# A four-block Mamba, sign and expert kernel: normalised outputs joined to the residual in one VectorE operation, their means carried to the end

## The reference

```python
x = x + _layernorm(_L0_attn_ref(_layernorm(x), ...))   # selective scan, 16 states
x = x + _layernorm(_L0_ffn_ref(_layernorm(x), ...))    # sign(x) @ sign(w).T, bias, alpha
x = x + _layernorm(_L1_attn_ref(_layernorm(x), ...))   # selective scan again
x = x + _layernorm(_L1_ffn_ref(_layernorm(x), ...))    # 16 experts, top 2, and 2 shared
```

## Time and profile before

| | us |
|---|---|
| median of 3 runs (791.62 to 793.70) | 792.56 |
| the profiled execution | 792.4 |
| its span | 790.5 |
| VectorE busy | 574.4 |
| TensorE busy (matmul) | 653.1 |

### The profile page before, as it was taken

The page is one execution under the profiler, slowest core; times in us unless marked ns, Lnnn a source line. Parts: engine busy times, 40 slices in busy tenths (PEclk is TensorE's granted clock), DMA queues, the critical chain, the costliest instruction groups (busy, mean ns, idle before and its releaser), DMA issues.

```text
span 790.5 us, 10083 instructions
## 1 busy us (share of the span) xinstructions
PE 653.1 (83%) x2907; PEld 417.3 (53%) x2909; DVE 574.4 (73%) x1137; ACT 542.5 (69%) x1213; POOL 453.2 (57%) x396
## 2 busy tenths in 40 slices
PE   3936999999994438648999999984989999999960
PEld 2325555555552324234555555543867777777640
DVE  6365999999997585649999999979583134444358
ACT  2769999999986775959999999956323322222225
POOL 0034999999994131048999999955047423333400
PEclk9956999999997577968999999995599999999986
DMA  6031444444430000012535444417012323333163
GB/s 165 6 67 36 133 140 133 140 133 142 131 115 1 0 1 3 18 58 94 149 118 160 134 134 149 131 46 231 1 54 94 105 96 107 106 105 103 64 219 107
DMA packets 57567, 77.65 MB, mean 98 GB/s; under 512 B 8113, under 2 KB 38481, under 8 KB 57521
## 3 DMA queue, kind: packets, MB, share of 16 engines
q1 hardware_dynamic: 53728, 66.75, 28.0%
q0 software_dynamic: 3792, 10.36, 3.7%
HBM read 58.21 MB, written 18.87 MB: 98 GB/s over the span
## 4 chain that ended last, share of the span: by engine, by line
PE 74%; DVE 13%; ACT 7%; POOL 3%; DMA 2%; issue 1%; SPq 0%; ACTq 0%; POOLq 0%; DVEq 0%
PE bank L1060 28%; PE bank L1050 14%; PE bank L1097 11%; DVE st L342 4%; PE bank L1105 3%; PE bank L1106 3%; PE bank L948 2%; PE bank L951 2%; POOL arena L896 2%; PE bank L961 2%; PE bank L934 2%; PE bank L970 2%; DVE tok_a L381 1%; ACT rings L793 1%; PE bank L1167 1%; DVE rings L686 1%
## 5 line engine op out<-in xcount | busy, mean ns | idle before, releaser
L881 POOL TENSOR_TENSOR arena<-arena,rings 128x512 f32<-128x512 f32 x256 | 321.6, 1283 | 31.3 <-DVE arena L510 26.9
L510 DVE TENSOR_TENSOR_SCAN arena<-rings,bank 128x512 f32<-128x512 f32 x256 | 296.2, 1200 | 15.9 <-PE bank L1050 7.1
L1060 PE MATMUL bank<-arena,ident 128*128 128x512 f32 x512 | 263.7, 601 | 0.0
L1050 PEld LDWEIGHTS bank<-ident,rings 128*128 128x128 f32 x1024 | 131.3, 145 | 143.8 <-issue 124.6
L793 ACT ACTIVATE rings<-tok_a,b_tok 128x256 f32<-128x256 f32 x448 | 191.0, 495 | 0.4 <-ACT tok_a L753 0.4
L803 ACT ACTIVATE rings<-arena,a_sb 128x512 f32<-128x512 f32 x256 | 169.1, 709 | 0.0
L1050 PE MATMUL bank<-ident,rings 128*128 128x128 f32 x1024 | 158.4, 280 | 11.3 <-ACT rings L793 10.9
L918 POOL DMA_INDIRECT y_tok<-rings,dest x47 | 44.9, 955 | 82.9 <-DVE rings L659 82.6
L1060 PEld LDWEIGHTS bank<-arena,ident 128*128 128x128 f32 x512 | 79.3, 193 | 5.7 <-issue 4.8
L857 ACT ACTIVATE silu<-bank 128x176 f32<-128x176 f32 x47 | 14.9, 317 | 85.5 <-PE bank L1097 85.5
L896 POOL TENSOR_TENSOR arena<-arena,feat_a 128x512 f32<-128x512 f32 x8 | 18.7, 2357 | 90.1 <-DVE arena L402 90.1
(11 more groups left out here) (160 smaller groups left out, 852.8 us busy)
## 6 DMA issues: line engine op xcount, KB each, us to landing
rings<-c_rows SPq DMA_DIRECT2D x128, 256.0 KB, 3.3
w_sb<-w SPq DMA_DIRECT2D x18, 352.0 KB, 4.1
x_sorted<-zeros SPq DMA_DIRECT2D x47, 128.0 KB, 3.2
rings<-x_sorted SPq DMA_DIRECT2D x47, 128.0 KB, 2.0
arena<-w SPq DMA_DIRECT2D x2, 2048.0 KB, 12.3
residual<-x SPq DMA_DIRECT2D x4, 512.0 KB, 6.1
tok_a<-y_tok SPq DMA_DIRECT2D x4, 512.0 KB, 7.3
w_sb<-y_tok SPq DMA_DIRECT2D x4, 512.0 KB, 8.1
```

The costliest lines, as they stand in the source:

```text
L510: dve.tensor_tensor_scan(state[:, u % STATE_RING, :], abar[:, u % ABAR_RING, :], bank[u % B_RING][:, :], 0.0, ALU.mult, ALU.add).then_inc( ...
L881: pool.tensor_tensor(s, s, crep[:, k % CREP_RING, :], ALU.mult).then_inc(hc_ready, 1)
L1050: ins = pe.transpose(bank[u % B_RING][:, j * P:(j + 1) * P], v_ring[:, s % V_RING, j, h * P:(h + 1) * P], ident[:, :])
L1060: pe.matmul(ysum_of[b % 2][h][:, :], ident[:, :], state[:, u % STATE_RING, :], start=n == 0, stop=n == N - 1).then_inc(state_free, 1)
```

## The change

In `y_add` and `r_add` VectorE adds `f * rstd` to X in one scalar_tensor_tensor per chunk; ScalarE's normalise and GpSimd's add go, and the term `-mean * rstd` is not added to X. The moments and reciprocals of these three norms are kept in buffers of their own. Since `mean * rstd` is one number for a token, the norms that read X are not changed by it; the sum of the three is formed once, in `carry`, ahead of the expert loops, and joined to the shift of the last norm (`m_norm`), which has one operation more. `x_norm` leaves only the reciprocal on VectorE, and GpSimd does the four tensor_scalar of a quarter. `f_mm` moves from VectorE to ScalarE, as an activation with scale alpha and bias `bias * alpha`, a product formed once after the first scan.

```diff
+            def add_scale(name, q, l):
+
+                g = slice(q * CQ, (q + 1) * CQ)
+                dve.wait_ge(std_ready, stat_of[q])
+                f, x_added = (f_tok[l - 1], y_added) if name == "y_add" else (f_tok[0], r_added)
+                rstd = moments(name, l)[1]
+                done(dve.reciprocal(rstd[:, g], std[:, g]))
+                settle()
+                for c in range(q * CQ, (q + 1) * CQ):
+                    dve.scalar_tensor_tensor(X[:, c, :], f[:, c, :], rstd[:, c:c + 1], X[:, c, :], ALU.mult, ALU.add)\
+                       .then_inc(x_added, 1)
...
-                if name != "x_norm":
+                if name == "f_norm":
                     dve.scalar_tensor_tensor(shift[:, g], mom[:, g, 0], -1.0, rstd[:, g], ALU.mult, ALU.mult)\
+                       .then_inc(scale_ready, 1)
+                elif name == "m_norm":
+                    done(dve.tensor_tensor(shift[:, g], mom[:, g, 0], rstd[:, g], ALU.mult))
+                    settle()
+                    dve.scalar_tensor_tensor(shift[:, g], shift[:, g], -1.0, carry[:, g], ALU.mult, ALU.subtract)\
                        .then_inc(scale_ready, 1)
...
                 elif name == "x_norm":
-                    scale(name, q)
-                    for c in range(q * CQ, (q + 1) * CQ):
-                        dve.tensor_scalar(tok_a[:, c, :], X[:, c, :], mom[:, c, 0:1], rstd[:, c:c + 1], ALU.subtract,
-                                          ALU.mult).then_inc(norm_ready, 1)
+                    dve.wait_ge(std_ready, stat_of[q])
+                    dve.reciprocal(rstd[:, g], std[:, g]).then_inc(x_scale_ready, 1)
...
-                elif name == "f_mm":
-                    for h in range(H):
-                        dve.wait_ge(ffn_ready, q * H + h + 1)
-                        dve.tensor_scalar(feat_a[:, h, t], bank[4 + h][:, :], bias_sb[:, h:h + 1], alpha_sb[:, h:h + 1],
-                                          ALU.add, ALU.mult).then_inc(scaled, 1)
...
+            done(dve.tensor_tensor(bias_sb[:, :], bias_sb[:, :], alpha_sb[:, :], ALU.mult))
...
+            done(dve.tensor_tensor(carry[:, :], kept_mom[0][:, :, 0], kept_rstd[0][:, :], ALU.mult))
+            for i in (1, 2):
+                settle()
+                done(dve.tensor_tensor(carry_part[:, :], kept_mom[i][:, :, 0], kept_rstd[i][:, :], ALU.mult))
+                settle()
+                done(dve.tensor_tensor(carry[:, :], carry[:, :], carry_part[:, :], ALU.add))
...
-                elif name in ("y_add", "f_norm", "r_add", "m_norm"):
+                elif name in ("f_norm", "m_norm"):
                     normalise(name, q, l)
...
+                elif name == "f_mm":
+                    for h in range(H):
+                        act.wait_ge(ffn_ready, q * H + h + 1)
+                        act.activation(feat_a[:, h, t], bank[4 + h][:, :], ACT.Identity, scale=alpha_sb[:, h:h + 1],
+                                       bias=bias_sb[:, h:h + 1]).then_inc(scaled, 1)
...
-                if name in ("y_add", "r_add"):
-                    f, f_normed, x_added = (f_tok[l - 1], y_normed, y_added) if name == "y_add" else (f_tok[0], r_normed, r_added)
+                if name == "x_norm":
+                    pool.wait_ge(x_scale_ready, l * Q + q + 1)
                     for c in range(q * CQ, (q + 1) * CQ):
-                        n = ((l - 1) * C if name == "y_add" else 0) + c + 1
-                        pool.wait_ge(f_normed, n)
-                        pool.tensor_tensor(X[:, c, :], X[:, c, :], f[:, c, :], ALU.add).then_inc(x_added, 1)
+                        pool.tensor_scalar(tok_a[:, c, :], X[:, c, :], mom[:, c, 0:1], rstd[:, c:c + 1], ALU.subtract,
+                                           ALU.mult).then_inc(norm_ready, 1)
```

More of the change, by code:

```diff
@@ L143, in sandwich_kernel @@
         rstd, shift = sb("rstd", [P, C]), sb("shift", [P, C])
+        kept_mom = [sb(f"kept_mom{i}", [P, C, 2]) for i in range(3)]
+        kept_rstd = [sb(f"kept_rstd{i}", [P, C]) for i in range(3)]
+        carry, carry_part = sb("carry", [P, C]), sb("carry_part", [P, C])
         eps_sb = sb("eps_sb", [P, 1])
@@ L179, in sandwich_kernel @@
         ftr_ready, ftr_copied = sem("ftr_ready"), sem("ftr_copied")
-        y_normed, r_normed, m_normed, y_added, r_added = (
-            sem(n) for n in ("y_normed", "r_normed", "m_normed", "y_added", "r_added"))
+        m_normed, y_added, r_added = (
+            sem(n) for n in ("m_normed", "y_added", "r_added"))
         g_normed = sem("g_normed")
@@ L233, in norm_of, with moments @@
         def norm_of(name, l):
-            return {"y_add": (f_tok[l - 1], f_tok[l - 1], y_normed), "f_norm": (tok_a, X, g_normed),
-                    "r_add": (f_tok[0], f_tok[0], r_normed), "m_norm": (f_moe, f_moe, m_normed)}[name]
+            return {"f_norm": (tok_a, X, g_normed), "m_norm": (f_moe, f_moe, m_normed)}[name]
+        def moments(name, l):
+            i = {"y_": 2 * (l - 1), "r_": 1}.get(name[:2])
+            return (mom, rstd) if i is None else (kept_mom[i], kept_rstd[i])
         block = ctx.enter_context(nc.Block())
@@ L333, in settle, with stat @@
                 dve.wait_ge(dve_done, steps[0])
-            def stat(src, q, ready=None, count=0, each=1):
+            def stat(src, q, ready=None, count=0, each=1, mom=mom):
                 for c in range(q * CQ, (q + 1) * CQ):
@@ L406, in stage @@
                 elif name == "y_stat":
-                    stat(f_tok[l - 1], q, ytr_copied, ((l - 1) * Q + q) * 2, 2)
-                elif name == "y_add":
-                    scale(name, q)
+                    stat(f_tok[l - 1], q, ytr_copied, ((l - 1) * Q + q) * 2, 2, moments(name, l)[0])
+                elif name in ("y_add", "r_add"):
+                    add_scale(name, q, l)
                 elif name == "f_stat":
@@ L423, in stage @@
                     scale(name, q)
-                elif name == "f_mm":
-                    for h in range(H):
-                        dve.wait_ge(ffn_ready, q * H + h + 1)
-                        dve.tensor_scalar(feat_a[:, h, t], bank[4 + h][:, :], bias_sb[:, h:h + 1], alpha_sb[:, h:h + 1],
-                                          ALU.add, ALU.mult).then_inc(scaled, 1)
                 elif name == "r_stat":
-                    stat(f_tok[0], q, ftok_copied, q * 2, 2)
-                elif name == "r_add":
-                    scale(name, q)
+                    stat(f_tok[0], q, ftok_copied, q * 2, 2, moments(name, l)[0])
                 elif name == "softmax":
@@ L701, in _, with root @@
             roots, norms = [0], [0]
-            def root(q):
+            def root(name, q, l):
                 g = slice(q * CQ, (q + 1) * CQ)
@@ L707, in root @@
                 act.wait_ge(var_ready, roots[0])
-                act.activation(std[:, g], mom[:, g, 1], ACT.Sqrt, bias=eps_sb[:, 0:1]).then_inc(std_ready, 1)
+                act.activation(std[:, g], moments(name, l)[0][:, g, 1], ACT.Sqrt, bias=eps_sb[:, 0:1]).then_inc(std_ready, 1)
             def normalise(name, q, l):
@@ L724, in stage @@
                 if name in ("x_stat", "y_stat", "f_stat", "g_stat", "r_stat", "m_stat"):
-                    root(q)
-                elif name in ("y_add", "f_norm", "r_add", "m_norm"):
+                    root(name, q, l)
+                elif name in ("f_norm", "m_norm"):
                     normalise(name, q, l)
```

1 line of the change is left out of this document (added).

## The result

The kernel after takes 815.15 us (median of 4 runs, 814.57 to 816.14) beside 792.27 us (now 4 runs, 791.62 to 793.7) before: ratio 1.0282 [1.0269, 1.0295], slower by 22.9 us. The forecast was 799.7 with a range to 806.5, so the direction is right and the size is wrong by 15 us. The profiled execution has a span of 813.0 us (before 790.5).

What follows compares the result with a forecast made beforehand. VectorE was taken to bound the norm stretches (ScalarE the middle one), delaying three starts of TensorE's work. Terms -0.55 + 4.7 + 2.4 + 0.6 = +7.15 us on the median 792.56 gave 799.7, range 794.0 to 806.5.

Steps and rivals of the forecast that it cites:

- The norm on GpSimd: Price of one x_norm operation moved to GpSimd: 0.5 us, 2.0 a quarter, with ends 0.24 and 0.73.
- Start A: Second quarter's transposes at the first norm, where TensorE's long work starts: 13.4 in place of 13.95 us, -0.55.
- B: Second quarter's transposes at the second norm stretch, 302.23 us before: 4.7 us later, with f_mm added to ScalarE.
- C: Second quarter's transposes at the third norm stretch: 550.9 in place of 548.46 us, +2.4.
- Slots: VectorE's fixed-order time per item: statistics 1.73 us, reciprocal 0.19, new add 1.77 a quarter, priced from L686's 0.40 each.
- rival of the dear add: The column-dependent part of each new VectorE add doubles: 15.4 us more over 48 adds, 815.1 us; chance 0.03.
- The shared access: VectorE's adds beside GpSimd's norm in the two later norm stretches: VectorE waits for one GpSimd operation, 0.4 us.
- strict turns: VectorE and GpSimd alternate on the shared access, so VectorE waits for four GpSimd operations, 1.5 us more.
- The rest: Carry hidden in VectorE's idle time, nothing (1 us uncovered); m_norm's extra operation 0.2 us a quarter, three exposed: +0.6.
- Slow and in turns: Rival: GpSimd's norm at 0.73 us with engines alternating in the later norm stretches: +15.7, 808.2 us; chance 0.12.
- The hand-overs count: Rival, faster: the new add replaces ScalarE's normalise and GpSimd's adds on the chain, -4.7 in all, 787.8 us; chance 0.10.
- Cheap on both: Rival, near no change: norm at 0.24 us, access free, f_mm at the copy's price: +1.95, 794.5 us; chance 0.10.

Runs made afterwards that it cites:

- e5_forms: Changed kernel with x_norm on GpSimd given other forms (one operation, constants, copy, 128x512) in quarters 1 to 3 of the first two norms; 813.48 us, one execution.
- e8_one_op: Changed kernel with the GpSimd norm cut to the subtraction only, 0.90 us an operation, scaling left out; ratio 1.0173 to the kernel before.
- e7_copy: Changed kernel with the GpSimd norm cut to a plain copy, 0.35 us an operation, normalisation left out; ratio 1.0094 to the kernel before.
- e2_norm_pool: Kernel before with only x_norm's tensor_scalar moved to GpSimd; 813.82 us, ratio 1.0259.
- e1_norm_dve: Changed kernel with x_norm's tensor_scalar back on VectorE, everything else kept; 802.89 us, ratio 1.0121 to the kernel before.
- e4_adds_only: Kernel before with only the joined add on VectorE and the means kept aside, x_norm and f_mm on VectorE; ratio 1.0144.
- e6_norm_act: Changed kernel with x_norm of the second and third block on ScalarE and of the first on VectorE; ratio 1.0132 to the kernel before.

## Why the prediction was right in sign and wrong in size

**The step that failed** is the price in "The norm on GpSimd": 0.5 us, with 0.24 and 0.73 as its ends. It measured 1.21. The lower end, a memset, and the upper one, the two-input add of the earlier trace rows, were taken as bounds because the norm reads one tensor where the add reads two. But e5_forms shows that the tensors read don't set the price: two operations with constants cost 1.04 us, one read and one write without arithmetic 0.35. A row with more inputs is no upper bound for another form, not even for one with a single operation (0.90). The trace before had no GpSimd operation with a per-partition operand or with two operations, and an upper end should have said so, say twice the add's 0.73, one for each operation.

**The same working with 1.21 us** gives the measured time, with two more numbers from the trace after, the gap between the reciprocals and the length of the eight operations. Start A: 9.3 + 8 x 1.21 = 19.0, +5.0. At B and C all eight stand in a row, since four (4.84) are longer than the 3.8 us between the two reciprocals (305.83 to 309.61, 559.26 to 563.04), so the start is q0's reciprocal + 9.7 + 0.5 (the eight take 10.20 us in the chain for 8 x 1.21 = 9.7): 304.8 - 3.8 + 10.2 = 311.2, +9.0, and 548.8 - 3.8 + 10.2 = 555.2, +6.7. With +0.6 for `m_norm` that is +21.3, or 813.9 beside 815.15. The forecast's form, in which only q1's four operations stand behind q1's reciprocal, holds for 0.5 us and fails with the price.

**Slots.** The new add has the price that L686 gave: four in 1.67 us at 555.94, 1.58 to the next operation. The rival of the dear add gave 815.1, almost the measured time, by a cost that isn't there: no run shows its doubling, which would make a quarter's slot some 2.9 us (1.58 + 4 x 0.32) where 1.58 was measured. A time that fits confirms no cause; the rows do.

**Start B and `f_mm`.** ScalarE in the middle stretch, kernel after:

```profile
272.51 2.07 ACT L738 ACTIVATE tok_a<-residual,shift,rstd 128x256 f32<-128x256 f32 x4 [0.18 <-DVE shift L381]
...
281.67 1.43 ACT L798 ACTIVATE feat_a<-bank,bias_sb,alpha_sb 128x512 f32<-128x512 f32 x2
283.00 2.07 ACT L738 ACTIVATE tok_a<-residual,shift,rstd 128x256 f32<-128x256 f32 x4
```

Less the 4.9 us of the later scan, the normalise of q1 is at 267.6 for 264.49: 3.1 later, forecast 3.05. The pair of `f_mm` has a slot of 1.33 us, as taken. q1's reciprocal at B, 309.61 less 4.9, is 304.7, forecast 304.8.

**The shared access.** At C the four adds beside the norm take 1.89 us for 1.67, and the first two norms 1.49 and 1.50 for 1.21: 0.2 for VectorE and 0.6 for GpSimd, where I had 0.4 for VectorE alone. Right in size, and strict turns, 1.5 us more for VectorE, didn't come. The traces show that both last longer side by side; what the two engines share no run shows. The forecast's "one operation of GpSimd, then four adds" isn't how it went: beside the shorter operations of e8_one_op and e7_copy the adds lost more, 0.4 and 0.6 us.

**The rest.** The carry's five operations stand at 621.49 to 622.49, in a stretch where VectorE waits for ScalarE, idle for 0.84 us just before them; they cost nothing. ScalarE's last eight normalises take 4.04 us as before. Behind C 1.2 us are lost for a forecast of 0.6, but e2_norm_pool, where `m_norm` is unchanged, also has 243.2, so about 1 us of that stretch isn't `m_norm`'s, and e1_norm_dve has 244.9; what it is stays open. TensorE's granted clock moved both ways, 0.69, 0.61, 0.67 and 0.63 for 0.58, 0.71, 0.66 and 0.63, and the eight transposes at each of the three starts take 1.97 us as before, so no gain of theirs stands in the time.

**The rivals.** "Slow and in turns" had the right direction for the norm's price, 0.73, but fell short by 7 us for want of the true one. "The hand-overs count" is refuted by e1_norm_dve and e4_adds_only: with the hand-overs gone and the norm on VectorE the kernel is still 1.2 to 1.4% slower. "Cheap on both" had the change near nothing with a cheap norm: with a copy in its place, at 0.35 us, it still loses 7.1 us.

## What to carry to other kernels

When an operation moves to an engine whose trace has no row of that form, take no row of another form as its upper bound, even one that touches more tensors (here the add at 0.73 us, where the norm took 1.21), and look first for the price from which it becomes the pace: here some 0.9 us, where four operations outlast the gap between two quarters. Before work leaves a busy engine, see that its new queue is idle at that moment and that nothing others wait for stands behind it, as ScalarE's copies did in e6_norm_act, for 1.1 us at B and at C. Where one engine is the bound, keep the part of an idea that takes work off it (the means kept aside, -0.4%), and leave the part that gives it more.

## What the runs showed of the hardware

- GpSimd on 128x256 f32: tensor_scalar 1.21 us with two operations and two per-partition operands, 1.04 with two and constants, 0.90 with one and one; a copy 0.35 (e5_forms); a two-input add 0.73. The form with two operations costs more than the form with two tensors, and so does its form with one operation.
- The same GpSimd operation has a spread of 1208 to 1213 ns from least to median, and up to 1504 beside VectorE's two-input adds. The quarter at the second norm of e5_forms that stands beside such adds has 5.37 us for 4.83.
- Both engines paid for that neighbourhood. VectorE's four adds, 1.67 us alone, took 1.89 beside operations of 1.21 us, 2.03 beside 0.90 (e8_one_op) and 2.25 beside copies of 0.35 (e7_copy), and those four copies took 2.01 for 1.41: the shorter GpSimd's operations, the more the adds lost.
